# Layer 1's heads, its feed-forward and layer 2's attention in one instruction order instead of three stages

## The chip, the cores and the metric

The kernel runs on one core of a Trainium2 chip. The metric is the time of one execution in device microseconds; the median of several runs counts. The engines of a core are TensorE (PE in the profile, its weight loads PEld), VectorE (DVE), ScalarE (ACT), GpSimd (POOL) and SyncE (SP), which only issues DMA transfers here. Each has its own instruction stream, works it off in order, and waits on semaphores that the others count up.

## The reference, cut to what matters

The reference is a transformer of four layers on `x` of 4 x 256 tokens and 256 features. The change touches three blocks and what joins them:

```python
x = x + _L1_attn_ref(_layernorm(x), ...)     # causal, 16 heads of 16
x = x + _L1_xattn_ref(_layernorm(x), ctx)    # 16 heads of 16 over 256 context tokens, int8 rounding of x, o and weights
x = x + _L1_ffn_ref(_layernorm(x), w1, b1, w2, b2)
x = x + _L2_attn_ref(_layernorm(x), ...)     # causal, 32 query heads of 8 in 8 groups

def _bitlinear(x, w, b):                     # in _L1_ffn_ref, twice, 256 -> 1024 -> 256, gelu between
    xn = _layer_norm(x)
    xq = _activation_quant(xn)               # rounded to 127 steps of the row's maximum
    wq = _weight_quant(w)                    # -1, 0, 1 times a scale
    return jnp.einsum('bsd,fd->bsf', xq, wq) + b
```

## The kernel before

The 1024 tokens are eight tiles of 128 (`NT = 8`), two to a batch. The kernel is a list of stages (`STAGES`). Each stage has one function for each engine, and each function ends with a drain and a count of `stage done`; no engine begins a stage before the other four engines' counts of the stage before are in. Semaphore names are reused from stage to stage (`Signals.next_stage`). Three stages matter here.

`L1Heads` (a `SmallHeads`) holds layer 1's self attention and cross attention as eight batches of four steps `s` of four heads. Time is counted in quarters `q` of a step. For each quarter every engine's function has a fixed list of work: score matmuls (`pe_scores`, three steps ahead), maxima on VectorE (`maximum`), the probabilities' matmuls (`pe_probabilities`, L1107), the exponential on ScalarE (L1296), the values (`pe_values`, L1134) and VectorE's copy of them (L1187). Projections ("units") and the rest of a batch come by two tables, `units` and `plan`: "turn" (transposes L1152, then division and int8 rounding of the rows on VectorE, L1264 to L292), "flip" (L1156, copied by ScalarE for even tiles, L1301, and by VectorE for odd ones, L1195), "project" (L1161, then the addition to x, L1199, and the statistics of the next normalisation, L230 and L232), and four quarters later the normalisation itself (`apply_next`, L247). The last step of heads is `s = 31`, quarters 124 to 127; after it only turns (quarters 132, 134), flips (136, 138), projections (140, 142) and normalisations (144, 146) are left for the last two tiles; the projections of the two tiles before stand in quarters 124 and 126. The quarters end at 147.

`L1Ffn` is a software pipeline over the eight tiles with `PHASES = 14`: step `n` does phase `n - t` for each tile `t`, 21 steps in all (0 to 20). Phase 0: statistics on VectorE (L1574, L1576) and their root on POOL. Phase 1: row scaling on VectorE (`rows`, L1609 to L1617) and two rounding passes on ScalarE (L1625, L1629). Phase 2: transposes (L1540) and their copy (L1633). Phase 3: the hidden products (L1547), scaled with the bias on VectorE (L1587), Gelu and squares on ScalarE (L1637, L1641). Phase 5: the rows of 1024 on VectorE (L1609, L1611) and ScalarE's rounding (L1647, L1649). Phase 6: eight transposes (L1555), copied by L1653. Phase 7: the out product (L1561) and its addition to x (L1598). Phases 8 and 9: statistics and normalisation for layer 2 (L230, L247). Phase 11: its transposes and their copy (`turn` L254 and L255, `keep` L260).

`L2Attn`, again a `SmallHeads`, has four batches of eight steps of four heads. Its quarters begin at -24: a key projection (L1067, eight matmuls) and four query projections, each split in bf16 parts by copies on ScalarE and VectorE (L1232) with matmuls between them (L1052), two value projections (L1706), the first scores in quarter -12 (L1080, L1087), their maxima (L1249), the first probabilities in quarter 1 (L1099, L1107).

In PSUM (eight banks) the heads use banks 0 and 1 for scores, 2 and 3 for probabilities, 4 for values, 5 and 6 for units and 7 for the rest. The feed-forward uses 0 for the first transposes, 1 and 2 for the hidden products, 3, 4 and 5. In SBUF the heads and both following stages use the area `K` from column 0 on.

SyncE's stream: layer 2's q, k, v and out weights are loaded at the start of the feed-forward's stage (`L1Ffn.sp`), nine further weights and the split parts at the start of the attention's (`L2Attn.sp`, 3072 KB for the latter).

## Time and profile before

| | |
|---|---|
| median of 3 runs | 2391.01 us (2387.65 to 2399.65) |
| profiled execution | 2393.9 us, of which 2392.0 from the first to the last instruction |
| mean granted TensorE clock | 0.913 |
| busy share: PE, DVE, ACT, POOL | 85%, 66%, 48%, 36% |
| heads' last step of heads to the end of their stage | about 706 to 731.2 us |
| feed-forward's stage | 731.3 to 807.1 us |
| layer 2's attention to its first probabilities | 807.1 to 840.9 us |

The rows below are of three kinds. A windows row gives for a stretch of the span how long each engine was busy in it. A timeline row is one instruction, or several alike merged (x with their number), with its start, its length, and in brackets how long its engine had been idle before it and what ended that. A row of the chain is a piece of the work that ended last. The granted clock is a share of 2.4 GHz: 1.00 is that level and 0.50 is 1.2 GHz.

### The profile page before, as it was taken

How to read it: one execution, taken by the hardware profiler on the slowest of the kernel's cores; microseconds unless marked ns; L12 is line 12 of the kernel's file. 1: busy time of each engine (PE TensorE's matmuls, PEld its weight loads, DVE VectorE, ACT ScalarE, POOL GpSimd, SP SyncE). 2: the span in 40 equal slices, each digit the busy share in tenths (PEclk: the TensorE clock that was granted, in tenths of full speed). 3: DMA queues.
4: the chain of work that ended last, by engine and by line, in shares of the span. 5: the costliest groups of instructions: out<-in, count | busy, mean ns of one | idle time of the engine just before them, and what ended most of it. 6: DMA issues, size and time to landing. Idle time of an engine off the chain costs nothing.

```text
span 2392.0 us, 38312 instructions
## 1 busy us (share of the span) xinstructions
PE 2024.2 (85%) x13444; PEld 1458.8 (61%) x13521; DVE 1572.8 (66%) x4123; ACT 1153.3 (48%) x2563; POOL 855.2 (36%) x1374
## 2 busy tenths in 40 slices
PE   6999957899994699965678999689999999997991
PEld 4888844566652356542255677368778787774770
DVE  4866567356657555645587888677888888765433
ACT  2357637234436534427376656145655655552330
POOL 3247851011113211211000000166776767664445
PEclk9999978899996789975689999899999999998996
DMA  6124430000000300010000000311111111125543
GB/s 259 45 76 143 150 108 1 1 2 2 2 2 28 153 1 2 2 38 1 0 1 1 1 1 1 143 54 40 45 41 58 41 41 45 45 96 165 117 137 103
DMA packets 57694, 130.96 MB, mean 55 GB/s; under 512 B 6657, under 2 KB 23553, under 8 KB 55521
## 3 DMA queue, kind: packets, MB, share of 16 engines
q1 hardware_dynamic: 52656, 115.80, 14.2%
q0 software_dynamic: 4560, 12.46, 2.4%
q8 instruction: 109, 1.79, 0.3%
q14 instruction: 81, 0.66, 0.1%
q10 hardware_dynamic: 288, 0.26, 0.0%
HBM read 100.31 MB, written 26.08 MB: 53 GB/s over the span
## 4 chain that ended last, share of the span: by engine, by line
PE 69%; DVE 13%; ACT 8%; issue 4%; POOL 4%; DMA 1%; SPq 1%; POOLq 0%; DVEq 0%; ACTq 0%; another core or an unknown queue 0%
PE ps L1067 4%; PE ps L2164 4%; PE ps L2505 4%; PE ps L2183 4%; PE ps L2527 3%; PE ps L1107 3%; PE ps L2551 3%; PE ps L2959 3%; PE ps L1087 3%; PE ps L1134 2%; PE ps L2559 2%; PE ps L2496 2%; PE ps L2487 2%; PE ps L2488 2%; PE ps L601 2%
## 5 line engine op out<-in xcount | busy, mean ns | idle before, releaser
L2815 POOL TENSOR_TENSOR K<-K 128x512 f32<-128x512 f32 x128 | 144.9, 1132 | 147.2 <-DVE K L2612 147.1
L1296 ACT ACTIVATE K<-ps 128x768 f32<-128x768 f32 (+1 forms) x128 | 110.7, 865 | 153.2 <-PE ps L1107 151.4
L2212 DVE TENSOR_TENSOR_SCAN W<-W,ps 128x512 f32<-128x512 f32 x128 | 155.7, 1217 | 40.0 <-issue 24.5
L2164 PEld LDWEIGHTS ps<-K 128*128 128x128 f32 x1024 | 136.6, 196 | 64.9 <-issue 51.0
L2755 ACT ACTIVATE K<-ps,K 128x256 f32<-128x256 f32 x128 | 60.8, 475 | 212.9 <-DVE K L2596 212.9
L2607 DVE TENSOR_SCALAR K<-ps,K 128x128 f32<-128x128 f32 x384 | 130.8, 402 | 27.1 <-POOL K L2832 26.8
L2164 PE MATMUL ps<-K 128*128 128x128 f32 x1024 | 139.2, 280 | 6.8 <-DVE W L2212 6.8
L2801 POOL TENSOR_SCALAR K<-K 128x1 f32<-128x1 f32 x16 | 3.6, 224 | 371.3 <-DVE K L2662 368.9
L1339 POOL CAST K<-K 128x8 bf16<-128x8 f32 x64 | 14.9, 233 | 330.8 <-issue 157.2
L2183 PE MATMUL ps<-W,C 128*128 128x512 f32 x256 | 132.2, 598 | 0.7 <-DVE W L2220 0.6
L2505 PE MATMUL ps<-K 128*128 128x256 f32 x512 | 131.8, 380 | 0.7 <-ACT K L2774 0.7
L237 POOL TENSOR_SCALAR Z<-Z 128x1 f32<-128x1 f32 x80 | 19.4, 242 | 313.4 <-DVE Z L232 313.4
L1249 DVE TENSOR_REDUCE K<-ps 128x2 f32<-128x256 f32 x192 | 97.9, 552 | 43.1 <-PE ps L1087 41.8
L2596 DVE TENSOR_REDUCE K<-ps 128x2 f32<-128x512 f32 x128 | 87.7, 685 | 51.7 <-PE ps L2488 51.4
L2374 ACT ACTIVATE W<-K 128x510 f32<-128x510 f32 x128 | 87.4, 714 | 39.9 <-DVE W L2212 39.7
L729 POOL TENSOR_TENSOR K<-K 128x512 f32<-128x512 f32 x64 | 66.8, 1044 | 105.5 <-DVE K L677 105.5
L2551 PE MATMUL ps<-W,K 128*128 128x512 bf16 x352 | 89.9, 391 | 8.9 <-DMA W<-split_weights 5.1
L1232 ACT ACTIVATE K<-ps 128x512 bf16<-128x512 f32 (+1 forms) x80 | 44.7, 560 | 107.9 <-PE ps L1067 65.5
L1107 PE MATMUL ps<-K 32*128 32x256 bf16 (+1 forms) x1536 | 95.3, 256 | 0.8 <-ACT K L1296 0.8
L2505 PEld LDWEIGHTS ps<-K 128*128 128x128 f32 x512 | 87.3, 190 | 7.6 <-ACT K L2768 1.0
L702 ACT ACTIVATE K<-ps,K 128x256 f32<-128x256 f32 x64 | 30.3, 473 | 123.1 <-DVE K L654 122.8
L2527 PE MATMUL ps<-W,C 128*128 128x256 bf16 x720 | 88.2, 273 | 0.0
(524 smaller groups left out, 5757.9 us busy)
## 6 DMA issues: line engine op xcount, KB each, us to landing
W<-split_weights SPq DMA_DIRECT2D x32, 768.0 KB, 4.4
split_weights<-W SPq DMA_DIRECT2D x40, 384.0 KB, 2.6
W<-in_m SPq DMA_DIRECT2D x32, 256.0 KB, 4.7
results<-K SPq DMA_DIRECT2D x63, 128.0 KB, 2.4
W<-split_weights SPq DMA_DIRECT2D x1, 5376.0 KB, 16.7
W<-in_wproj SPq DMA_DIRECT2D x16, 256.0 KB, 3.0
W<-in_m SPq DMA_DIRECT2D x32, 128.0 KB, 5.6
W<-split_weights SPq DMA_DIRECT2D x1, 3072.0 KB, 20.3
```

What stands on the lines that cost most here:

```text
L1067: m = t.e.matmul(bank[:, i * 256:(i + 1) * 256], W[:, k, (c + i) * 128:(c + i + 1) * 128], x[:, k, b * 256:(b + 1) * 256], start=i == 0 an ...
L1107: m = t.e.matmul(self.probabilities_bank(b, j, k), y[:, k * 128:k * 128 + 128], x[:, q0:256], start=i == 0 and not self.causal(b), stop=i ...
L1249: m = e.tensor_reduce(to[:, :, i:i + 1], banks.rearrange("p (j k) -> p j k", j=2)[:, :, c0:c1], AX.X, ALU.max, negate=True)
L1296: e.activation(to, made, ACT.Exp, scale=self.SCALE).then_inc(*self.up("exp"))
L2164: m = e.matmul(ps[1 + 2 * (n % 2)][:, b * 128:(b + 1) * 128], self.dtuT[h][:, i, b * 128:(b + 1) * 128], self.diag[s % 4][:, b * 128:(b + ...
L2183: e.matmul(ps[4 + i][:, :], g.ident, self.y[(n - 3) % 5], start=False, stop=s == 15).then_inc(*sig.up("m total"))
L2212: e.tensor_tensor_scan(self.st[i % 3], self.a[i % 3], ps[1 + 2 * (i % 2)][:, :], 0.0, ALU.mult, ALU.add).then_inc(*sig.up("m scan"))
L2505: m = e.matmul(ps[6][:, 0:256], V[:, k, (i // 2) * 128:(i // 2 + 1) * 128], T[:, k * 256:(k + 1) * 256], start=k == 0, stop=k == 1)
L2527: m = e.matmul(ps[7][:, a * 256:(a + 1) * 256], self.o8[n % 3][:, i * 256 + a * 128:i * 256 + (a + 1) * 128], W[:, p * 512 + i * 256:p * 5 ...
L2551: m = e.matmul(bk[:, :], xs[:, cross, k, (j - 1) * 128:j * 128], W[:, p * 512:(p + 1) * 512], start=k == 0 and p == 0, stop=k == 1 and p == 2)
L2607: m = e.tensor_scalar(o[:, hs], ps[2 + u % 2][:, hs], mv[:, h, 0:1], r[:, h:h + 1], ALU.subtract, ALU.mult)
L2815: e.tensor_tensor(Pv, Pv, st[:, 4:6].unsqueeze(2).to_broadcast([128, 2, 256]), ALU.mult).then_inc(*sig.up("x scaled"))
```

## The change

The three stages become one, `Layers`, with one instruction order for all engines. The heads' quarters run as before; after the quarters named in `EARLY` one step of the feed-forward follows (step 0 after quarter 124, up to step 6 after quarter 145). Steps 7 to 11 follow the heads. From step 12 on (`BESIDE`) three quarters of layer 2's heads stand behind each step, so quarters -24 to 2 stand beside steps 12 to 20. The other quarters follow. The engine functions `pe`, `dve`, `act` and `pool` of `SmallHeads` and `L1Ffn` are split in a part before the loop (`dve_begin` and so on) and one for a single quarter or step (`pe_at` and so on); what they issue for it is unchanged. The feed-forward moves to buffers and PSUM banks that the heads no longer use (its first transposes to bank 2, hidden products to 0 and 1, the last transposes to 7; buffers in `W` and at the end of `K`), with waits that these are free. The loads of layer 2's q, k, v and out weights wait for the heads' last unit, the nine further loads and the split parts for the last tile's normalisation and its transposes.

```diff
-    LEAD, NB = 3, B
+    LEAD, NB, NAME = 3, B, "heads "
...
-        a, spare, more = Area(g.K, 0, WKCOLS), Area(g.W, 11264, 14336), Area(g.W, 2048, 4096)
+        a, spare, more = Area(g.K, 0, 17460), Area(g.W, 11264, 14336), Area(g.W, 2048, 4096)
...
-    def __init__(self, g):
-        self.g, self.sig, self.ps = g, g.sig, g.ps
-        a = Area(g.K, 0, 20020)
-        self.st, self.sc = a.new(NT, 2, 16), a.new(NT, 2, 4)
-        self.r1, self.rq, self.rqT = a.ring(2, 256), a.ring(3, 256, dt=BF16), a.ring(3, 2, 128, dt=BF16)
-        self.rh, self.rt = a.ring(4, 1024), a.ring(3, 1024)
-        self.squares = a.new(1024, dt=BF16)
-        self.rg, self.rgT = a.ring(3, 1024, dt=BF16), a.ring(3, 8, 128, dt=BF16)
+    def __init__(self, g, heads):
+        self.g, self.sig, self.ps, self.heads = g, g.sig, g.ps, heads
+        a, b, c = Area(g.W, 4096, 9216), Area(g.W, 14336, 19456), Area(g.K, 17460, 20020)
+        self.rh = a.ring(4, 1024)
+        self.st, self.sc, self.r1 = a.new(NT, 2, 16), a.new(NT, 2, 4), a.ring(2, 256)
+        self.rt, self.squares, self.rg = b.ring(3, 1024), b.new(1024, dt=BF16), b.ring(3, 1024, dt=BF16)
+        self.rq, self.rqT, self.rgT = c.ring(3, 256, dt=BF16), c.ring(3, 2, 128, dt=BF16), c.ring(3, 8, 128, dt=BF16)
...
-    def steps(self):
-        for step in range(NT + self.PHASES - 1):
-            for t in range(max(0, step - self.PHASES + 1), min(NT, step + 1)):
-                yield t, step - t
-
-    def sp(self, d):
+    STEPS = NT + PHASES - 1
+
+    def tiles(self, step):
+        return [(t, step - t) for t in range(max(0, step - self.PHASES + 1), min(NT, step + 1))]
+
+    def sp(self, d, heads):
+
+        d.wait_ge(heads.s("unit"), len(heads.made))
         for name in ("wq2", "wk2", "wv2", "wo2"):
             self.g.load(d, name)
 
-    def pe(self, t):
+    def pe_at(self, t, step):
         g, sig, ps, e = self.g, self.sig, self.ps, t.e
-        t.wait_ge(sig["w ternary"], 64)
-        for i, ph in self.steps():
+        for i, ph in self.tiles(step):
             if ph == 2:
                 t.wait_ge(sig["l1f rows"], i + 1)
                 t.wait_ge(sig["l1f kept"], i)
-                pb = ps[0].bitcast(BF16)
+                t.wait_ge(self.heads.s("exp"), 2 * self.heads.N)
+                pb = ps[2].bitcast(BF16)
                 for k in range(2):
                     m = e.transpose(pb[:, k * 128:(k + 1) * 128], self.rq[i % 3][:, k * 128:(k + 1) * 128], g.identb)
                 m.then_inc(*sig.up("l1f turned"))
             elif ph == 3:
+                t.wait_ge(sig["w ternary"], 64)
                 t.wait_ge(sig["l1f kept"], i + 1)
                 t.wait_ge(sig["l1f biased"], 2 * i)
+                t.wait_ge(self.heads.s("maximum"), 2 * self.heads.N)
                 for c in range(2):
                     for k in range(2):
-                        m = e.matmul(ps[1 + c][:, :], self.rqT[i % 3][:, k, :], self.w1[:, k, c * 512:(c + 1) * 512],
+                        m = e.matmul(ps[c][:, :], self.rqT[i % 3][:, k, :], self.w1[:, k, c * 512:(c + 1) * 512],
                                      start=k == 0, stop=k == 1)
                     m.then_inc(*sig.up("l1f hidden"))
...
+                t.wait_ge(self.heads.s("quad kept"), self.heads.N)
...
-                g.norms[6].turn(t, i, ps[5])
-
...
+    NAME = "heads of 8 "
+
     def sp(self, d):
+
+        nx = self.g.norms[6]
+        d.wait_ge(self.sig[nx.name + " xnT"], nx.tbase + NT)
+        d.wait_ge(self.sig["l1f x"], NT)
...
+        t.wait_ge(self.sig[g.norms[6].name + " xnT"], g.norms[6].tbase + 2 * b + 2)
...
+class Layers:
+
+
+
+    EARLY = {124: 0, 126: 1, 129: 2, 132: 3, 136: 4, 140: 5, 145: 6}
+    BESIDE = 12
+
+    def __init__(self, g):
+        self.g, self.sig = g, g.sig
+        self.heads = L1Heads(g)
+        self.ffn = L1Ffn(g, self.heads)
+        self.attn = L2Attn(g)
+
+    def order(self):
+
+        for q in self.heads.quarters:
+            yield "heads", q
+            if q in self.EARLY:
+                yield "ffn", self.EARLY[q]
+        first, behind = max(self.EARLY.values()) + 1, list(self.attn.quarters)
+        for step in range(first, self.ffn.STEPS):
+            yield "ffn", step
+            if step >= self.BESIDE:
+                for q in behind[3 * (step - self.BESIDE):3 * (step - self.BESIDE) + 3]:
+                    yield "attn", q
+        for q in behind[3 * (self.ffn.STEPS - self.BESIDE):]:
+            yield "attn", q
+
+    def heads_ended(self, eng):
+
+        h, nx = self.heads, self.g.norms[5]
+        eng.wait_ge(h.s("rest"), max(h.made_rest.values()))
+        eng.wait_ge(h.s("kept"), len(h.number))
+        eng.wait_ge(h.s("quads"), h.N)
+        eng.wait_ge(h.s("quad kept"), h.N)
+        eng.wait_ge(h.s("logits"), 2 * h.N)
+        eng.wait_ge(h.s("exp"), 2 * h.N)
+        eng.wait_ge(h.s("unit"), len(h.made))
+        eng.wait_ge(h.s("parts"), h.N // 2)
+        eng.wait_ge(h.s("quantised"), NT)
+        eng.wait_ge(self.sig[nx.name + " xn"], nx.base + NT)
+
+    def banks_free(self, t, q):
+
+        nx = self.g.norms[6]
+        if q >= -4 * self.attn.LEAD:
+            t.wait_ge(self.sig["l1f biased"], 2 * NT)
+        if q >= -1:
+            t.wait_ge(self.sig["l1f kept"], NT)
+            t.wait_ge(self.sig["l1f hidden kept"], NT)
+            t.wait_ge(self.sig["l1f x"], NT)
+            t.wait_ge(self.sig[nx.name + " xnT"], nx.tbase + NT)
+
+    def sp(self, d):
+        self.heads.sp(d)
+        self.ffn.sp(d, self.heads)
+        self.attn.sp(d)
+
+    def pe(self, t):
+        for stage, n in self.order():
+            if stage == "heads":
+                self.heads.pe_at(t, n)
+            elif stage == "ffn":
+                self.ffn.pe_at(t, n)
+            else:
+                if n == self.attn.quarters[0]:
+                    self.heads_ended(t)
+                self.banks_free(t, n)
+                self.attn.pe_at(t, n)
+
...
-STAGES = [(1, L0Attn), (3, L0Cross), (5, L1Heads), (6, L1Ffn), (7, L2Attn), (8, L2Cross), (9, L2Moe),
+STAGES = [(1, L0Attn), (3, L0Cross), (7, Layers), (8, L2Cross), (9, L2Moe),
...
```

The functions `dve`, `act` and `pool` of `Layers` follow the same order as its `pe`.

## Rows read from the trace of the kernel before

**Rows 1.** The page's part 1, busiest engine: busy us, share, instructions.
```profile
PE 2024.2 (85%) x13444; PEld 1458.8 (61%) x13521; DVE 1572.8 (66%) x4123; ACT 1153.3 (48%) x2563; POOL 855.2 (36%) x1374
```

**Rows 2.** Windows: length, busy PE, PEld, DVE, ACT, POOL, granted clock, DMA share, GB/s.
```profile
706.00:731.40 25.40, 16.34 (x96) 8.63 (x92) 10.92 (x33) 3.46 (x4) 3.29 (x8) 0.63 0.00 1
731.40:762.00 30.60, 11.68 (x49) 5.16 (x50) 24.18 (x71) 21.51 (x36) 11.98 (x24) 0.52 0.15 54
762.00:793.00 31.00, 18.11 (x93) 10.29 (x94) 27.79 (x69) 29.96 (x49) 10.76 (x24) 0.67 0.00 1
793.00:807.10 14.10, 8.12 (x52) 5.18 (x49) 8.01 (x23) 9.06 (x13) 3.33 (x8) 0.76 0.01 2
807.10:825.80 18.70, 11.85 (x48) 8.09 (x49) 3.54 (x10) 6.62 (x11) 1.88 (x6) 1.00 0.95 372
825.80:840.90 15.10, 10.05 (x87) 4.58 (x88) 7.87 (x16) 2.22 (x4) 1.93 (x10) 0.71 0.37 145
840.90:858.00 17.10, 16.75 (x133) 8.66 (x133) 6.40 (x12) 4.65 (x6) 1.92 (x10) 0.55 0.00 1
```

**Rows 3.** Timeline, the heads' last quarters: start us, length us, instruction, [idle before].
```profile
713.55 0.42 DVE L1199 TENSOR_TENSOR X<-ps,X 128x256 f32<-128x256 f32 x1 [0.99 <-PE ps L1161]
...
714.47 0.18 DVE L232 BATCH_NORM_AGGREGATE Z<-Z 128x2 f32<-128x6 f32 x1
...
714.53 1.02 ACT L1296 ACTIVATE K<-ps 128x1024 f32<-128x1024 f32 x1 [3.27 <-PE ps L1107]
...
717.98 0.26 DVE L1264 RECIPROCAL K<-ps 128x16 f32<-128x16 f32 x1 [0.49 <-PE ps L1152]
...
720.23 0.25 DVE L1264 RECIPROCAL K<-ps 128x16 f32<-128x16 f32 x1
...
723.94 2.08 PE L1161 MATMUL ps<-W,K 128*128 128x256 f32 x4 [0.58 <-DVE K L1195]
```

**Rows 4.** Timeline, feed-forward, the first instructions of some steps.
```profile
733.14 0.80 DVE L1609 TENSOR_SCALAR K<-W,K 128x256 f32<-128x256 f32 x1 [1.06 <-POOL K L1666]
...
735.13 0.42 DVE L1574 BATCH_NORM_STATS2 K<-W 128x6 f32<-128x256 f32 x1
...
735.31 0.60 ACT L1625 ACTIVATE K<-K,Z 128x256 f32<-128x256 f32 x1 [13.21 <-DVE K L1581]
...
745.44 1.54 DVE L1587 SCALAR_TENSOR_TENSOR K<-ps,K,C 128x512 f32<-128x512 f32 x2 [2.43 <-PE ps L1547]
...
749.04 0.78 DVE L1609 TENSOR_SCALAR K<-K 128x1024 f32<-128x1024 f32 x1
...
755.28 0.78 DVE L1609 TENSOR_SCALAR K<-K 128x1024 f32<-128x1024 f32 x1
...
761.98 0.48 DVE L1598 SCALAR_TENSOR_TENSOR X<-ps,K,X 128x256 f32<-128x256 f32 x1
```

**Rows 5.** Timeline, feed-forward from its step 12 on.
```profile
795.64 1.03 PE L1555 MATMUL ps<-Cb,K 128*128 128x128 bf16 x8 [1.85 <-ACT K L1649]
...
798.89 1.15 ACT L1649 ACTIVATE K<-K,Z 128x1024 bf16<-128x1024 f32 x1
...
802.25 1.05 PE L1561 MATMUL ps<-W,K 128*128 128x256 bf16 x8 [0.69 <-ACT K L1653]
...
806.67 0.38 ACT L260 ACTIVATE K<-ps 128x256 f32<-128x256 f32 x1 [0.79 <-PE ps L255]
```

**Rows 6.** Timeline, layer 2's attention until its first probabilities.
```profile
807.14 1.99 PE L1067 MATMUL ps<-K,W 128*128 128x256 f32 x8 [0.51 <-ACTq L3426]
...
815.27 1.89 PE L1067 MATMUL ps<-K,W 128*128 128x256 f32 x8
...
825.82 0.32 PEld L1080 LDWEIGHTS ps<-Cb 128*128 128x128 bf16 x2
...
840.89 0.82 PE L1107 MATMUL ps<-K 32*128 32x256 bf16 x8
```

**Rows 7.** The chain that ended last, a projection in layer 2's second batch.
```profile
852.63 3.69 PE ps L1067 x8
```

More of the change, by code:

```diff
@@ new lines, in pe_at @@
+    def pe_at(self, t, q):
+        s, p, second = q // 4, q % 4 // 2, q % 2
+        if not second and 0 <= s + self.LEAD < self.N:
+            self.pe_scores(t, s + self.LEAD, p)
+        if second and 0 <= s < self.N:
+            self.pe_probabilities(t, s, p)
+        for u, kind, b, c, n in self.units.get(q, ()):
+            if n == 0:
+                if u >= 2:
+                    self.wait_part(t, u - 2, self.last[u - 2])
+                m = self.unit(t, kind, b, c, self.ps[5 + u % 2])
+            else:
+                self.wait_part(t, u, n - 1)
+                t.wait_ge(self.s("minus"), 1)
+                m = t.e.matmul(self.ps[5 + u % 2][:, :], self.minus[self.levels(kind, b)[n - 1][2]], self.part(u, kind, b, c, n - 1),
+                               start=False, stop=True, skip_group_check=True)
+            m.then_inc(*self.up("unit"))
+        if q % 4 == 1 and 0 <= s - 1 < self.N:
+            self.pe_values(t, s - 1)
+        for kind, b, c, u in self.plan.get(q, ()):
+            t.wait_ge(self.s("kept"), u)
+            m = self.pe_rest(t, kind, b, c)
+            if kind != "norm":
+                m.then_inc(*self.up("rest"))
@@ L1310, in pool, with pool_begin @@
+    def pool_begin(self, p):
         e = p.e
@@ L1563, in pe, with dve_at @@
             elif ph == 11:
-                g.norms[6].turn(t, i, ps[5])
-    def dve(self, v):
+                t.wait_ge(self.heads.s("kept"), len(self.heads.number))
+                g.norms[6].turn(t, i, ps[7])
+    def dve_at(self, v, step):
         g, sig, ps, e = self.g, self.sig, self.ps, v.e
         xn = g.norms[5].xn
-        for i, ph in self.steps():
+        for i, ph in self.tiles(step):
             s0, s1, c0, c1 = self.st[:, i, 0, :], self.st[:, i, 1, :], self.sc[:, i, 0, :], self.sc[:, i, 1, :]
@@ L1618, in rows, with act_at @@
         v.wait_ge(v.own, v.n)
-    def act(self, a):
+    def act_at(self, a, step):
         g, sig, ps, e = self.g, self.sig, self.ps, a.e
-        for i, ph in self.steps():
+        for i, ph in self.tiles(step):
             if ph == 1:
@@ L1655, in act, with pool_at @@
             elif ph == 11:
-                g.norms[6].keep(a, i, ps[5])
-    def pool(self, p):
+                g.norms[6].keep(a, i, ps[7])
+    def pool_at(self, p, step):
         g, sig, e = self.g, self.sig, p.e
-        for i, ph in self.steps():
+        for i, ph in self.tiles(step):
             s0, s1 = self.st[:, i, 0, :], self.st[:, i, 1, :]
```

205 lines of the change are left out of this document (109 added, 96 removed).

## The prediction, made before the change was run

> **What bounds the kernel now.** I read the page first. TensorE is busy 85% of the span [rows 1], but that is a mean over stages, and the change touches only the stretch from the heads' last quarters to the first quarters of layer 2's attention. So I cut that stretch into windows [rows 2] and ask of each which engine has no room. In the heads' tail (706 to 731.4) VectorE works 10.9 of 25.4 us and ScalarE 3.5: a chain of small steps from engine to engine, with room on both. In the feed-forward's filling steps (to 762) VectorE works 24.2 of 30.6. In its full steps (to 793) ScalarE works 30.0 of 31.0 and VectorE 27.8: ScalarE is the bound and there is nothing to win. From 793 to 807 the pipeline drains, all engines below two thirds. Then layer 2's projections (to 825.8) are again a chain: VectorE 3.5 and ScalarE 6.6 of 18.7 us. From 825.8 on TensorE and VectorE hand one score bank pair to and fro. The change lays the filling steps over the heads' tail, and the draining steps over the projections. Both overlaps are of latency-bound work with latency-bound work on in-order engines, so what counts is not the sum of busy times but what each inserted piece makes the next one wait for.
>
> **The change, part by part: the front.** I follow VectorE, which is the slower engine here, from quarter 126. Nothing before it changes: step 0 is two short statistics instructions. Quarter 126's addition starts at 713.55 and its statistics end at 714.65 [rows 3], so an addition with statistics costs 1.1.
>
> Step 1 is new behind it. One tile's row scaling takes 2.0 (733.14 to 735.13), and the next tile's statistics 0.6 [rows 4]: 2.6 together. ScalarE, in order, has to do its part of step 1 before the exponential of quarter 127. The scale is ready at 716.7, ScalarE's two passes take 1.1, so that exponential starts at about 717.9 where it started at 714.53 [rows 3]: 3.4 late. TensorE's values and VectorE's copy of them queue behind it. Step 2 stands behind quarter 129 and adds 2.6 on VectorE, of which 0.4 fell into idle time. So quarter 132's row work starts at 723.6, not 717.98: 5.6 late. It takes 2.3 (717.98 to 720.23) [rows 3].
>
> From here on the rest is a sum on VectorE: 725.9; step 3, as long as step 4 was before (745.44 to 749.04, 3.6) [rows 4]: 729.5; quarter 134's rows 2.3: 731.8; step 4, 3.6 and 0.4 of wait for its hidden products, which stand behind the flip of quarter 136 on TensorE: 735.8; quarter 138's copy 0.4: 736.2; wait for the projection of quarter 140, 2.1 of TensorE [rows 3] and the hand-over, 2.5: 738.7; addition and statistics 1.1: 739.8; step 5 6.2 (749.04 to 755.28) [rows 4]: 746.0; quarter 142 1.1 and the normalisation of quarter 144 0.4: 747.5; step 6 6.7 (755.28 to 761.98): 754.2; the last normalisation 0.4: 754.6. Before, step 7 began at 761.98 [rows 4]. The front gives 7.4. The whole tail disappears as a stage of its own, but its work does not: from 706 to 762 VectorE has 35.1 us of work [rows 2].
>
> Its bounds: from 713.55 to 762 VectorE works about 34 of 48.4 us (35.1 of [rows 2], less about 1.4 that stand before 713.55); its chains of dependent short instructions leave some 4 of gaps which nothing fills. So the front gives 11 at the very most. At the least: if each inserted step costs its old time including its waits, only steps 0 to 2 (731.4 to about 739.3) fall into idle time, less the 5.6 by which they delay quarter 132: 2.
>
> **Steps 7 to 11** keep their pace: ScalarE is full [rows 2].
>
> **The tail.** TensorE finished step 12 at 796.67 and ScalarE at 800.04 [rows 5]; both come 7.4 earlier, 789.3 and 792.6. The 27 quarters of the next heads go in threes behind steps 12 to 20. The first key projection (2.0 [rows 6]) can run while ScalarE is in step 12, but its copy waits for ScalarE until 792.6, 1.3 later than on an idle engine. From this projection to the next but one took 8.1 before (807.14 to 815.27) [rows 6]. Now TensorE has in addition step 13 (a turn 0.4, the out product 1.05, eight transposes 1.03 [rows 5]) and step 14 (0.4 and 1.05). About 0.7 of step 13 lies in the time in which TensorE would wait for the copy. Sum: 789.3 + 8.1 + 1.3 + 2.5 - 0.7 + 1.5 = 802.0 for the second query projection. Step 13's copy on ScalarE (1.0) goes ahead of the keys' last copies, but these are done before the chain needs them. From there to the first scores took 10.6 (815.27 to 825.82) [rows 6], plus 0.4 for one turn that is in nobody's shadow: 813.0. The old time was 825.82. From the scores to the first probabilities took 15.1 (to 840.89) [rows 6]. The last turns lie in TensorE's waits for the maxima; I add 0.5 for a maximum that comes behind the last normalisation. So by the chain alone the first probabilities start at 828.6, 12.3 earlier. The draining stage from 796.67 to 807.05 [rows 5] was 10.4 long, and I get 5 of it: the rest is paid back as TensorE work inside the new chain.
>
> **Edits costed at nothing.** The Q, K, V, out weights of layer 2 are loaded earlier, the nine big loads and the split parts later by at most the length of the draining steps; the first reader of the latter is a stage away, and DMA is idle before it. The new waits (the heads' counters, the free banks) are met: each is counted up at least a step before. The exponential's table is still left once and taken again once, since the last exponential stands ahead of step 3 and the first new one behind step 10. POOL works under 40% everywhere here [rows 2]. Two stage borders go, 0.2 us.
>
> **The clock** is the term that no row settles. The granted clock was 1.00, the level of 2.4 GHz, in the projections (807 to 825.8), though TensorE was busy only 11.9 of 18.7 us, and between the two levels (0.76) in the drain before it [rows 2]. The same eight matmuls take 1.89 at the high level [rows 6] and 3.69 in the stretch of 0.55 [rows 7, 2]. Now the projections start at 789.3, where the clock was at the low level. TensorE is busier here than in the old drain, so I expect the high level after the first or second projection. One slow projection is half hidden by ScalarE, the second is not: 1.5 lost. Bounds: nothing, if it rises at once; if it never does, five projections at 1.8 more (9.0, 1.3 of it hidden), the value projections 1.0, three pairs of scores 0.5 each: 11.
>
> Here the Trainium skill (TensorE: Matmul & The Clock Gate, Part 1: The HAM clock gate) speaks for the change's second half. It says that the slow level is the default and that sustained work on the array releases it. By it the filled gaps would keep the clock up and the 1.5 would not be lost. The trace agrees that the projections ran at 1.00, but it also shows a busy array at 0.55 from 840.9 to 858 (16.8 of 17.1 us) [rows 2], so I keep the 1.5.
>
> **Sum:** 12.3 - 1.5 = 10.8 earlier, and nothing after this stretch changes. The profiled execution took 2393.9 us (span 2392.0); the median of the runs is 2391.0. I take the gain off the median: **2380.2 us**, 0.45% less. A measurement of this kernel can tell about 0.5% (12 us) from no change, so the forecast lies just inside.
>
> **Rivals.**
> *Full overlap.* The inserted steps fit into idle time almost everywhere: front 11, tail 10 (the whole drain). For it: VectorE's 10.9 of 25.4 and ScalarE's 3.5 in the tail [rows 2]. Against it: the 3.4 us by which the exponential of quarter 127 is late, and TensorE's in-order work at each step border. 21 less: 2370. With half of the difference to my sum, 2375.
> *The in-order engines give it back.* Each inserted step waits for a result that is just being made, and the quarter behind it waits too. Front 2, tail 1: 2388. For it: the waits of 2.4 and 1.06 that the filling steps showed [rows 4].
> *Slower, by the clock.* The low level holds from 790 through the projections (11 lost, which leaves 1.3 of the gain) and lasts longer under the first quarters that follow. There TensorE is busy 16.75 of 17.1 us at 0.55 [rows 2]: the work would take half the time at full clock. If as much of such work again is done at the low level, 8.5 more: 2398. It decides from about 3 us of saturated work at the low level beyond the stretch that was slow before. Against it: the projections alone brought 1.00 before.
>
> **How the numbers follow.** Forecast 0.54, full overlap 0.24, given back 0.13, slower by the clock 0.09. The forecast's own range is 2375 to 2386, and two fifths of it lie beyond 0.5%. So faster by over 0.5%: 0.24 and 0.21 of the forecast, 0.45. Slower by over 0.5% (above 2403) takes two such stretches: 0.05. Within: 0.50. The range reaches to full overlap on one side and to the case that gives it back on the other: 2369 to 2391.
>
> **What the new profile would show.** The exponential of quarter 127 3 to 4 us after 714.5; the first Gelu near 727, not 741; step 7 on VectorE near 755; the full steps still 7.1 apart; the first key projection near 789 to 790, and 12 to 14 us from it to the second query projection, where it was 8.1; the first scores near 813 to 815; the first probabilities near 829 to 831; granted clock 1.00 from about 795 to 820; after it the same pace to the end. Wrong would be: step 7 not before 759 (the front's chain), or projections of 3.7 us each after 797 (the clock), or a low stretch behind the first probabilities much longer than 17 us, or a wait for a weight in the stages after.

## The result and the profile after

The changed kernel's median is 2371.82 us (nine runs, 2366.25 to 2385.55), against 2391.18 us (nine runs, 2387.65 to 2403.75) for the kernel before on the same chip. The ratio is 0.9921, with a 95% interval of 0.9903 to 0.9939: 19.4 us, or 0.8%, faster. The forecast was 2380.2, a gain of 10.8. Its direction was right, the time lies in its range, and the gain was sized at little more than half; the case "faster by over 0.5%", which came, had been given 0.45.

The profiled execution took 2366.25 us (span 2364.3), the fastest of its nine. The one of before took 2393.9 (span 2392.0), near the middle of its own. So the two profiles differ by 27.7 us, more than the kernels do, and the first task is to say which part belongs to the change. The page's part 1 has the same work as before, instruction for instruction on TensorE [rows 1]; its matmuls are busy 17 us less:

```profile
PE 2007.2 (85%) x13444; PEld 1451.7 (61%) x13521; DVE 1571.2 (66%) x4123; ACT 1152.4 (49%) x2563; POOL 857.4 (36%) x1374
```

Three names are used from here on. The front is the stretch on VectorE from quarter 126's addition to the first instruction of step 7, the tail the stretch from there to the first probabilities on TensorE, and the low level a granted clock of 0.50 (1.2 GHz). Windows of the changed kernel, with the columns of [rows 2]: the heads' last quarters with steps 1 to 6 beside them; the full steps; the draining steps beside layer 2's projections; from its first scores to its first probabilities; the stretch behind. The fence ends with three shorter stretches of the same core, of which the granted clock is what matters.

```profile
704.30:742.70 38.40, 19.14 (x102) 10.21 (x102) 31.74 (x97) 23.41 (x40) 13.82 (x29) 0.73 0.00 0
742.70:773.50 30.80, 16.90 (x91) 9.53 (x94) 28.16 (x71) 29.82 (x48) 11.16 (x24) 0.68 0.00 1
773.50:802.50 29.00, 21.21 (x96) 15.10 (x96) 10.63 (x31) 13.73 (x21) 5.39 (x14) 0.81 0.00 1
802.50:817.00 14.50, 9.95 (x89) 4.75 (x88) 7.69 (x15) 3.37 (x7) 1.93 (x10) 0.71 0.55 201
817.00:834.00 17.00, 16.61 (x154) 8.80 (x154) 8.42 (x16) 5.25 (x7) 2.16 (x12) 0.75 0.92 367
...
788.60:807.90 19.30, 13.80 (x94) 9.34 (x93) 8.26 (x19) 8.24 (x17) 2.05 (x5) 1.00 0.00 0
808.00:824.90 16.90, 13.69 (x111) 5.48 (x111) 7.11 (x14) 3.76 (x5) 3.86 (x20) 0.52 0.94 368
825.20:832.00 6.80, 6.41 (x70) 3.84 (x69) 3.92 (x8) 2.22 (x3) 0.00 (x0) 0.97 1.02 397
```

Where the heads' tail had VectorE at 10.9 of 25.4 us and the filling steps at 24.2 of 30.6 [rows 2], one stretch now has it at 31.74 of 38.40. The full steps are as long as before.

The timeline of the same stretch (VectorE, ScalarE and one TensorE row), to set beside [rows 3] and [rows 4]. L1200 is the addition that was L1199, L1265 the reciprocal that was L1264, L1299 the exponential that was L1296, L1619 the row scaling that was L1609, L1608 the addition that was L1598:

```profile
704.35 0.42 DVE L1200 TENSOR_TENSOR X<-ps,X 128x256 f32<-128x256 f32 x1 [0.61 <-PE ps L1160]
705.37 0.38 DVE L1619 TENSOR_SCALAR W<-W 128x256 f32<-128x256 f32 x1
...
707.70 0.51 ACT L1639 ACTIVATE K<-W,Z 128x256 bf16<-128x256 f32 x1
708.12 1.00 ACT L1299 ACTIVATE K<-ps 128x1024 f32<-128x1024 f32 x1
...
709.17 1.60 PE L1133 MATMUL ps<-K,W 128*32 128x256 f32 x16 [3.88 <-ACT K L1299]
...
713.62 0.25 DVE L1265 RECIPROCAL K<-ps 128x16 f32<-128x16 f32 x1
...
719.34 0.23 DVE L1265 RECIPROCAL K<-ps 128x16 f32<-128x16 f32 x1
...
725.33 0.39 DVE L1196 COPY K<-ps 128x256 f32<-128x256 f32 x1
...
725.77 1.26 PE L1160 MATMUL ps<-W,K 128*128 128x256 f32 x4 [2.66 <-DVE K L1196]
...
727.08 0.42 DVE L1200 TENSOR_TENSOR X<-ps,X 128x256 f32<-128x256 f32 x1 [1.36 <-PE ps L1160]
...
728.10 0.78 DVE L1619 TENSOR_SCALAR W<-W 128x1024 f32<-128x1024 f32 x1
...
736.14 0.80 DVE L1619 TENSOR_SCALAR W<-W 128x1024 f32<-128x1024 f32 x1
...
742.72 0.48 DVE L1608 SCALAR_TENSOR_TENSOR X<-ps,W,X 128x256 f32<-128x256 f32 x1
```

Read it with quarter 126's addition as zero. It stands at 704.35, and stood at 713.55 [rows 3], and but for step 0's two short statistics the instructions ahead of it are the same in both kernels: these 9.2 us are not the change's. Most of them are older than the heads' end. The addition of layer 1's first projection on VectorE shows it, in the kernel before and in the changed one:

```profile
513.92 0.42 DVE L1199 TENSOR_TENSOR X<-ps,X 128x256 f32<-128x256 f32 x1 [1.76 <-PE ps L1161]
...
507.80 0.42 DVE L1200 TENSOR_TENSOR X<-ps,X 128x256 f32<-128x256 f32 x1 [1.76 <-PE ps L1160]
```

So 6.1 us were there 200 us ahead of the change, and nearly all of that arises between 350 and 480 us, where the two executions had another granted clock. The same window of both, before and after:

```profile
395.00:460.00 65.00, 44.97 (x260) 29.46 (x263) 25.86 (x64) 25.22 (x39) 9.07 (x30) 0.76 0.00 1
...
395.00:460.00 65.00, 44.67 (x318) 29.89 (x320) 26.10 (x65) 26.26 (x41) 10.74 (x39) 0.89 0.00 1
```

The other 3.1 us come near the end of the heads, where the stretch at the low level was 3.4 us long in this execution and 10.2 in that of before. From the zero of quarter 126's addition, the exponential of quarter 127 starts 3.77 later (0.98 before), TensorE waits 3.88 for it, quarter 132 begins after 9.3 us, quarter 134 after 15.0, and step 7 after 38.37. That last figure was 48.43 before [rows 3, 4].

TensorE's timeline from the first projection of layer 2 on, to set beside [rows 6]:

```profile
776.22 2.75 PE L1066 MATMUL ps<-K,W 128*128 128x256 f32 x8
...
783.08 3.62 PE L1066 MATMUL ps<-K,W 128*128 128x256 f32 x8
...
786.92 1.61 PE L1570 MATMUL ps<-W,K 128*128 128x256 bf16 x8
788.37 0.61 PE L1563 MATMUL ps<-Cb,W 128*128 128x128 bf16 x8
...
791.51 1.89 PE L1066 MATMUL ps<-K,W 128*128 128x256 f32 x8
...
802.50 0.38 PE L1079 MATMUL ps<-Cb 128*128 128x256 bf16 x2
...
816.99 0.61 PE L1098 MATMUL ps<-Cb 128*128 128x256 bf16 x2
...
827.89 1.35 PE L1066 MATMUL ps<-K,W 128*128 128x256 f32 x5
```

The first projection has moved to 33.5 us behind step 7, where it was 45.2 [rows 4, 6]. The third comes 15.3 us behind the first (8.1 before), since step 13's out product and transposes, and step 14, stand between the second and the third, and since the first two run at 2.75 and 3.62 us, not 1.99 and 1.89. From step 7 to the first probabilities it is 74.3 us; in the profile of before it was 78.4, from 761.98 to the first pair of products of L1099:

```profile
840.35 0.61 PE L1099 MATMUL ps<-Cb 128*128 128x256 bf16 x2
...
852.56 3.76 PE L1067 MATMUL ps<-K,W 128*128 128x256 f32 x8
```

So of the 27.7 us between the two profiles 9.2 lie ahead of the change. 10.1 come from its front and 4.1 from its tail. The rest, 4.3, lies behind it, 1.3 of that between the first probabilities and the next batch's first projection (10.9 us, and 12.2 before, 840.35 to 852.56), where the stretch at the low level was 17.1 us long here and 23.9 there. Two profiles alone give the change 14.2 us. The timed runs give it 19.4. That difference is what most of the experiments are about.

### The profile page after: what moved, and what is told of

The parts are those of the page before. It is cut to its first block, busy times and chain, and to the rows that moved or that the text cites. A ratio compares the mean times of both kernels' runs of the same rounds, so it can differ in the third digit from the quotient of the medians.

```text
span 2364.3 us, 38312 instructions
## 1 busy us (share of the span) xinstructions
PE 2007.2 (85%) x13444; PEld 1451.7 (61%) x13521; DVE 1571.2 (66%) x4123; ACT 1152.4 (49%) x2563; POOL 857.4 (36%) x1374
## 4 chain that ended last, share of the span: by engine, by line
PE 68%; DVE 14%; ACT 7%; issue 5%; POOL 4%; DMA 1%; SPq 1%; POOLq 0%; another core or an unknown queue 0%; DVEq 0%; ACTq 0%
PE ps L2632 4%; PE ps L2291 4%; PE ps L1066 4%; PE ps L2310 4%; PE ps L2654 3%; PE ps L2678 3%; PE ps L1106 3%; PE ps L3086 3%; PE ps L1086 3%; PE ps L1133 2%; PE ps L2686 2%; PE ps L2623 2%; PE ps L2614 2%; PE ps L2615 2%; PE ps L601 2%
## 5 line engine op out<-in xcount | busy, mean ns | idle before, releaser
L1299 ACT ACTIVATE K<-ps 128x768 f32<-128x768 f32 (+1 forms) x128 | 110.7, 865 | 145.5 <-PE ps L1106 143.8
L1106 PE MATMUL ps<-K 32*128 32x256 bf16 (+1 forms) x1536 | 93.8, 253 | 0.8 <-ACT K L1299 0.8
```

Of the source, the lines that this page charges most:

```text
L1106: m = t.e.matmul(self.probabilities_bank(b, j, k), y[:, k * 128:k * 128 + 128], x[:, q0:256], start=i == 0 and not self.causal(b), stop=i ...
L1299: e.activation(to, made, ACT.Exp, scale=self.SCALE).then_inc(*self.up("exp"))
```

## The experiments

No kernel leaves work out. The "spare matmuls" of some are products whose results nothing reads.

**One half at a time, neither, and one step later.**

e1_front_only keeps the early steps and puts all of layer 2's quarters behind the feed-forward:

```
-    BESIDE = 12
+    BESIDE = 21
```

> Feed-forward steps 0 to 6 in the heads' last quarters as in the change, but layer 2's quarters all behind step 20 (BESIDE = 21). Theory A (two chains, each shortened by its own overlap, as in the prediction; the sizes as the changed kernel's trace has them): this keeps the front's 10 us, so about 2381, ratio 0.996; the addition of quarter 126 to VectorE's step 7 takes 38 us as in the changed kernel, and the projections run from the drain's end at the high clock. Theory B (the gain beyond 10.8 us is the clock's, because work beside the drain keeps TensorE busy): front alone gives the predicted 7 or less, 2384 or more. Theory C (the front gives nothing that the tail does not need): 2390.

e2_tail_only keeps the overlap behind step 12 and starts the feed-forward after the heads:

```
-    EARLY = {124: 0, 126: 1, 129: 2, 132: 3, 136: 4, 140: 5, 145: 6}
+    EARLY = {}
...
-        first, behind = max(self.EARLY.values()) + 1, list(self.attn.quarters)
+        first, behind = max(self.EARLY.values(), default=-1) + 1, list(self.attn.quarters)
```

> All feed-forward steps behind the heads (EARLY empty), layer 2's quarters beside steps 12 to 20 as in the change. Theory A: the tail alone gives 3 to 5 us, about 2387, ratio 0.998; from the last transposes of the draining pipeline to the first probabilities about 41 us where it was 44. Theory B: the tail is the larger half and this kernel is 9 or more faster, 2382 or less, with a shorter low stretch of the clock behind the first scores (17 us, not 25).

e3_neither makes both edits: the new code in the old order.

> One stage with neither overlap (EARLY empty, BESIDE = 21): only the other banks and buffers, the earlier loads and the missing stage borders remain. Both theories: within 3 us of the kernel before, 2388 to 2392. A rival (the borders, buffers and banks carry part of the gain): 2384 or less.

e4_step1_after_127 lets the exponential of quarter 127 go ahead of step 1:

```
-    EARLY = {124: 0, 126: 1, 129: 2, 132: 3, 136: 4, 140: 5, 145: 6}
+    EARLY = {124: 0, 127: 1, 129: 2, 132: 3, 136: 4, 140: 5, 145: 6}
```

> The changed kernel with feed-forward step 1 behind quarter 127 in place of 126, so that ScalarE's exponential of quarter 127 stands ahead of it. Theory A (the prediction's step: that exponential is 3.4 us late and everything to quarter 132 with it): the exponential starts 1.0 us after the addition of quarter 126 instead of 3.8, quarter 132's rows 2.5 to 3 us earlier, the kernel 2 to 3 us faster than the changed one, 2369. Rival (VectorE is full from there on and takes the time back): same as the changed one, 2372.

All four ran on one chip, where the kernel before had a median of 2395.27 us in 24 runs (2385.97 to 2403.67). The last two columns are read from each kernel's profile, from quarter 126's addition to step 7 and from there to the first probabilities:

| kernel | median (runs) | ratio, 95% | front | tail |
|---|---|---|---|---|
| front only | 2381.04 (8) | 0.9939, 0.9917 to 0.9961 | 39.5 | 84.2 |
| tail only | 2389.59 (12) | 0.9965, 0.9944 to 0.9985 | 48.1 | 72.3 |
| neither | 2393.54 (12) | 1.0002, 0.9982 to 1.0022 | 48.1 | 84.7 |
| step 1 after 127 | 2371.25 (6) | 0.9905, 0.9873 to 0.9937 | 36.4 | 73.7 |

The new code in the old order is the kernel before, as far as 12 runs can tell (5 us either way): what the change moves in memory and in its waits shows no cost. The halves add up within their intervals: 0.9939 times 0.9965 is 0.9904, and the whole is 0.9921 with an interval that holds it. The front is worth 9 to 10 us by the profiles (48.1 to 48.5 in the old order, 37.4 to 39.5 in the new) and 14.6 by its ratio, of which the interval, 9.3 to 19.9, just holds the other reading. The tail is worth 8.4 by its ratio (3.6 to 13.4). The forecast had 7.4 and 3.4. Neither half gives back what the other wins. Against what was expected of these kernels: front only came out at the 2381 of theory A, but its projections did not run at the high level, as that theory had it (3.62 and 3.16 us for the first two). Tail only was to be 3 to 5 us faster; its ratio gives more, its median 5.7.

The step behind quarter 127 confirms the reading of the late exponential. It starts 0.98 after the addition again, as in the kernel before; ScalarE's timeline of that run has it ahead of step 1's pass, and the addition was at 717.37:

```profile
718.35 1.02 ACT L1299 ACTIVATE K<-ps 128x1024 f32<-128x1024 f32 x1 [3.57 <-PE ps L1106]
720.08 0.60 ACT L1635 ACTIVATE W<-W,Z 128x256 f32<-128x256 f32 x1 [0.71 <-DVE W L1591]
```

Step 7 comes 2.0 us sooner after quarter 126 than in the change (36.4 for 38.4). In the total, 2 us can't be told from nothing by six runs: 0.9905 against 0.9921 with overlapping intervals, and 2371.25 us where 2369 was expected.

**The kernel before, twice more.** The table already says something that the first profile did not: neither and front only, both with the old tail, took 84.7 and 84.2 us for it, not 78.4. To see whether that is the new code or the execution, the kernel before was run and profiled again, unchanged, as g2_before_again and g3_before_again.

> The kernel before, profiled again. The claim: the profile that the prediction used had layer 2's first projections at the high clock (1.99 and 1.89 us), which is not how this kernel mostly runs; here the first two take 3.2 to 3.7 us and the way from VectorE's step 7 to the first probabilities is 84 us, not 78. Rival: 1.9 and 78 again, and the low level in the two kernels with the old order (front only, neither) came from their other buffers and borders.

> The same once more, for the same question: the first two projections 3.2 to 3.7 us by the claim, 1.9 by the rival. The low stretch near the end of the heads (10 us in the first profile, 3 to 14 in the later ones) should be there again, with another length.

They took 2398.30 and 2402.91 us, with 83.4 and 81.6 us from step 7 to the first probabilities. Windows of the first of them, the feed-forward's draining steps, the first two projections, and the rest of the projections:

```profile
791.20:805.80 14.60, 10.15 (x50) 6.14 (x48) 7.75 (x22) 8.17 (x12) 3.12 (x8) 0.50 0.01 2
...
807.40:816.30 8.90, 7.37 (x17) 5.04 (x18) 1.44 (x7) 1.20 (x2) 1.87 (x6) 0.52 0.88 342
816.40:829.60 13.20, 8.30 (x35) 5.09 (x34) 2.08 (x3) 5.43 (x9) 0.00 (x0) 1.00 1.03 412
```

and TensorE's timeline of it, with an out product and the first three projections:

```profile
800.88 1.89 PE L1561 MATMUL ps<-W,K 128*128 128x256 bf16 x8 [0.69 <-ACT K L1653]
...
807.39 3.78 PE L1067 MATMUL ps<-K,W 128*128 128x256 f32 x8 [0.51 <-ACTq L3426]
...
813.71 3.01 PE L1067 MATMUL ps<-K,W 128*128 128x256 f32 x8
...
818.82 1.89 PE L1067 MATMUL ps<-K,W 128*128 128x256 f32 x8
```

The same out product took 1.05 and the first projections 1.99 and 1.89 in the first profile [rows 5, 6], with a granted clock of 0.76 in the drain and 1.00 behind it [rows 2]. Here the drain is at 0.50, the low level, and the rise comes only at 816. Nothing in the code differs. In g3_before_again the first projection took 3.44 and the second 1.89; with neither it was 3.62 and 3.24, with the front only 3.62 and 3.16. Over the five profiles of the old tail without spares (78.4, 83.4, 81.6, 84.7, 84.2) the mean is 82.5 us, and the profile on which the forecast was built is the shortest of the five. The other four, though, were taken in executions whose time lies above the median: 2398.30, 2402.91, 2400.17 for neither (median 2393.54) and 2398.36 for front only, the longest of its eight. So the mean may lie above what a median execution has. Against that, a short time does not need a short tail: one kernel of the old order below, with spare matmuls in its drain, was profiled at 2387.39 us and has 82.2 us there, and its quarter 126 at 705.07. Over the five of the new tail with no spares between step 7 and the first scores (74.3, 72.3 with the tail only, 73.7 with step 1 behind 127, and 73.3 and 73.4 in two kernels below) the mean is 73.4, and they lie within 2 us.

**Is the gain only the clock's?** If a longer stay at the high level were what the change gains, a kernel that is held there should gain nothing by the new order. Spare matmuls were put where TensorE idled:

```
+    def fill(self, t, bank, n):
+        x = self.g.identb.rearrange("p (i n) -> p i n", i=1).to_broadcast([128, 4, 128])
+        for _ in range(n):
+            t.e.matmul(self.g.ps[bank][:, :].rearrange("p (i n) -> p i n", n=128), self.g.identb, x, start=True, stop=True,
+                       skip_group_check=True)
```

f1_fill_scores puts three of them behind seven of the quarters that make layer 2's first scores, in the changed kernel:

```
+                if n in (-12, -10, -8, -6, -4, -2, 0):
+                    t.wait_ge(self.sig["l1f kept"], NT)
+                    self.fill(t, 2, 3)
```

> The changed kernel with three spare matmuls (128x512 bf16, identity by identity, result never read) behind the score matmuls of quarters -12, -10, ... 0 of layer 2's heads, where TensorE waits for the maxima. It tests whether the granted clock behind the first scores is a term of time that the kernel's own gaps set. Clock theory: the low stretch of 17 to 24 us there goes, TensorE was full in about 16 us of it, so 7 to 8 us faster than the changed kernel (about 2364), and the spread of the runs shrinks. Rival (the clock follows something else, or the spare work costs what it gives): 2372 or more, low stretch still there.

f3_fill_heads puts two to four behind eleven of the heads' last quarters (quarter: bank and number), each time with a wait for the last maxima, and from quarter 130 on for the last exponentials, which read those banks:

```
+    FILL = {117: (0, 2), 119: (0, 4), 127: (0, 4), 128: (0, 4), 130: (3, 2), 131: (3, 2), 133: (3, 4), 135: (3, 4), 137: (3, 3), 139: (3, 3), 141: (3, 3)}
```

> The changed kernel with two to four spare matmuls behind eleven of the heads' quarters from 117 to 141, where TensorE waits for VectorE or ScalarE. Clock theory: the low stretch of 3 to 14 us at the end of the heads goes (full TensorE work there, worth up to 5 us) and the projections of quarters 140 and 142 take 1.1 instead of 2.1: 3 to 5 us faster than the changed kernel, 2368. Rival (spare matmuls at full TensorE cost more than they give): 2373.

f4_fill_all has both, and four behind each of the feed-forward's steps 10 to 12:

```
+                if n in (10, 11, 12):
+                    self.fill(t, 6, 4)
```

> Both sets of spare matmuls, and four more behind each of the feed-forward's steps 10, 11 and 12, in the changed order. Clock theory: the sum, 12 us faster than the changed kernel, about 2360, runs within 6 us of one another. Rival: no better than the better one of the two parts.

f5_neither_fill_all is the old order with the same spares, and four behind each of steps 2 to 20:

```
+                if n in range(2, 21):
+                    self.fill(t, 6, 4)
```

> The old order (EARLY empty, BESIDE = 21) with the same spare matmuls in the heads and the scores, and four behind each of the feed-forward's steps 2 to 20, so that the clock stays high where it matters in this order too. What is left between this kernel and the changed order with spare matmuls is the gain without the clock. Theory A (both overlaps shorten chains, 9 to 10 us in front and 4 to 5 in the tail): 14 us above it, about 2374. Theory B (half of the measured 19 us is the clock that stays high longer in the changed order): 10 us or less above it, about 2370. Theory C (the clock is no part at all): 19 above it.

All four ran on one chip (kernel before: 2393.28 in 15 runs). The last column is the time at the low level between 640 and 900 us:

| kernel | median (runs) | ratio, 95% | front | tail | low level |
|---|---|---|---|---|---|
| f1 | 2368.04 (5) | 0.9897, 0.9863 to 0.9931 | 38.6 | 73.3 | 71.7 |
| f3 | 2373.36 (5) | 0.9914, 0.9881 to 0.9947 | 37.4 | 73.4 | 64.8 |
| f4 | 2365.20 (5) | 0.9879, 0.9845 to 0.9913 | 38.1 | 72.1 | 37.5 |
| f5, old order | 2383.93 (11) | 0.9953, 0.9935 to 0.9972 | 47.0 | 81.2 | 37.5 |

For comparison, the changed kernel had 71.7 us at the low level there, the kernel before 102.4, 112.6 and 119.5 in its three profiles.

f4 and f5 spend the same 37.5 us at the low level, and the new order is still 18.7 us faster by the medians (15.8 by the means). Ten or less had been expected if half of the gain were the clock's, fourteen if both overlaps shorten chains by what had been read so far, nineteen if the clock had no part. The two ratios leave some 9 us either way (an estimate from their intervals), so that ten lies at the edge of what they allow, and fourteen and nineteen can't be told apart. That counts against the clock as the main source of the gain, but less cleanly than it looks, since the spares cost the old order something too. Windows of f5, from step 7 to the first scores and from there to the first probabilities; and below them those of f4, where the first begins with the draining steps:

```profile
750.70:818.50 67.80, 47.56 (x256) 27.81 (x255) 40.84 (x100) 45.15 (x70) 15.70 (x37) 0.90 0.30 116
818.50:831.90 13.40, 12.01 (x106) 5.51 (x105) 8.04 (x16) 2.33 (x4) 1.94 (x10) 1.00 0.26 99
```

```profile
779.40:807.50 28.10, 19.11 (x102) 13.59 (x101) 12.37 (x36) 14.36 (x21) 5.00 (x14) 0.94 0.00 0
807.50:820.70 13.20, 12.17 (x110) 5.93 (x109) 8.24 (x17) 3.48 (x7) 1.93 (x10) 1.00 0.46 173
```

The clock is at 0.90 and above in both, and from the scores on it takes 13.4 and 13.2 us. In f5 all projections take 1.89, and yet its tail is 81.2, longer than the 78.4 of the first profile of before.

g4_neither_fill_drain asks for this cost alone: the old order, with four spares behind each of steps 10 to 20 and none elsewhere.

```
+                if n in range(10, 21):
+                    self.fill(t, 6, 4)
```

> The old order in one stage (neither overlap) with four spare matmuls behind each of the feed-forward's steps 10 to 20 and nowhere else: TensorE is busy in the drain. If the low clock of the first projections costs the old order 5 to 6 us, this gives it back: all projections at 1.9, step 7 to the first probabilities 78 to 80 us instead of 84.7, about 2388 against 2394, ratio to before 0.997 to 0.998. Rival (the old order mostly runs its projections at the high level anyway, or the spare work costs as much): 2393 or more, ratio 1.000.

It ran at 2394.71 us (12 runs; kernel before 2392.78 in 17), ratio 1.0005, 0.9986 to 1.0024: the expected gain did not come. TensorE's timeline shows both sides of the bargain:

```profile
799.36 2.75 PE L1826 MATMUL ps<-Cb 128*128 128x512 bf16 x12
801.95 1.24 PE L1066 MATMUL ps<-K,W 128*128 128x256 f32 x5
```

The first projection is at the high level (so are the four behind it, 1.89 each), but it stands behind twelve spares, 2.75 us of them, and comes 48.8 us after step 7, where it came after 45.2, 47.1 and 47.1 in the three profiles of the kernel before. What the clock gives in the projections the spares take in the drain, in part at least: 82.2 us for the tail, against 84.7 with neither in its one profile and a total that is the same. In the drain the old order has nothing useful to put where the spares go; the new order has the projections.

The spares behind the first scores are different. f1's timeline of TensorE:

```profile
807.54 0.81 PE L1826 MATMUL ps<-Cb 128*128 128x512 bf16 x3
...
819.80 0.38 PE L1098 MATMUL ps<-Cb 128*128 128x256 bf16 x2
820.11 0.50 PE L1106 MATMUL ps<-K 32*128 32x256 bf16 x8
...
827.51 1.35 PE L1066 MATMUL ps<-K,W 128*128 128x256 f32 x5
```

They lie in TensorE's waits for VectorE's maxima, and there is no low stretch any more: the window from 806.5 to 827.5 has a granted clock of 1.00. From the first probabilities to the next batch's projection it takes 7.7 us, where it took 10.9 in the change and 11.2 to 12.2 in every other profile with the low level there; the eight products of L1106 take 0.50, not 0.82. From the first scores on that is 21.0 us for 25.4, 4.4 won where 7 to 8 had been expected. In the total, f1's 2368.04 lies between the 2364 of the clock theory and the 2372 of its rival, and its ratio can't be told from the change's (0.9897 and 0.9921, overlapping intervals). The spares in the heads did what they were put there for (none of the four kernels that have them shows the low stretch ahead of quarter 126's addition, of 3.4 to 13.7 us in all others), but the ratio of f3 shows no gain from it: 2373.36 us, its rival's 2373 and not the 2368 of the clock theory. Nor did the sum come: f4 was to run at 2360 with all runs within 6 us, and ran at 2365.20 with runs from 2363.11 to 2373.61.

**The best version.** g1_best is f4 with step 1 behind quarter 127 and spares behind step 9 too:

```
-    EARLY = {124: 0, 126: 1, 129: 2, 132: 3, 136: 4, 140: 5, 145: 6}
+    EARLY = {124: 0, 127: 1, 129: 2, 132: 3, 136: 4, 140: 5, 145: 6}
...
+                if n in (9, 10, 11, 12):
+                    self.fill(t, 6, 4)
```

> The changed order with all spare matmuls (heads, feed-forward steps 9 to 12, scores) and step 1 behind quarter 127. Clock theory and the in-order term add: 1 to 2 us below the kernel with all spare matmuls, 2363 to 2366, ratio to before 0.987 or 0.988. Rival: the two do not add, 2368 or more.

2365.48 us (6 runs, 2364.03 to 2369.70), ratio 0.9887, 0.9864 to 0.9909. Front 36.1, tail 71.6, 34.1 us at the low level. f4 (0.9879) and g1 can't be told apart. By medians both are some 6 us below the changed kernel, by ratios 8 to 10, and their ratios' intervals just overlap with its own, so that this further step is likely, not certain. Against the kernel before both intervals lie well below 1.

## Why the prediction was right in direction and short in size

**The front: 7.4 forecast, 9 to 10 measured.** The chain was followed rightly and every term came out a little shorter. With quarter 126's addition as zero: quarter 132 forecast at 10.05, found at 9.3 (the exponential 3.8 behind the zero, so 2.8 later than before, not 3.4); quarter 134 at 15.95, found at 15.0; the copy of quarter 138 at 22.25, found at 21.0; the addition of quarter 140 at 25.15, found at 22.7; step 7 at 41.05, found at 38.37. The largest single miss is the wait for quarter 140's projection: 2.5 forecast with the 2.08 of [rows 3] in it, 1.36 found, since the four matmuls ran faster (1.26). The price of that row came from a stretch at the low level. The full steps kept their pace (30.2 us for steps 7 to 11, 31.1 before), and the exponential's delay went where it was said to go, into TensorE's wait. Undoing it gave the 2.0 us of e4.

**The tail's chain: right in length.** From step 7 to the first scores the forecast gives 58.4 and 1.5 for the clock, 59.9. Found: 59.7, to their weight load as the forecast counts. That it fits so closely is partly luck: two errors of 1.2 or so offset each other: the first projection came 1.2 sooner behind step 7 than forecast, and the third 15.3 behind the first, outside the 12 to 14 that were named. From the scores to the probabilities (counted to the second of their products, L1106 at 817.52, as the forecast counted) it took 15.1 us for 15.6.

**The clock: the term that failed.** The forecast took 1.5 off the gain, because the new projections might begin at the low level while those of before ran at the high one. The first half of the thought was right: the two first ones took 2.75 and 3.62 us, and measured from step 7 the clock was at 1.00 from 45 us on (forecast 40) until 66 (forecast 65). The second half was read from one execution. In the other profiles of the old order, those of g2, g3, e1 and e3, the old projections begin at the low level as well, and the drain ahead of them is at 0.50, not 0.76 [rows 2]. That makes the old tail 81.6 to 84.7 us where the forecast had 78.4. The step of the prediction that failed is its sentence that the granted clock was 1.00 in the projections, used as a property of the kernel: it was a property of that run. So the clock gave something to the change, where 1.5 had been taken off. Its worst case for the clock, 11 lost, is also added up wrongly: 9.0 with 1.3 of it hidden, 1.0 and 1.5 make 10.2.

**The sum, set right:** 10.8, and 2.7 for the front (38.4 for 41.05), and 1.6 for the new tail (73.4 for 75.0, counted to the first of the probabilities' products, the clock's 1.5 included), and 4.1 for the old tail (82.5 for 78.4): 19.2, against 19.4 measured. The last term rests on five profiles that spread over 6 us, four of them of executions that took longer than the median, and is known to 1 or 2 us at best; that the sum comes out so near is no proof of it. The first two terms do not depend on it.

Here the Trainium skill (TensorE: Matmul & The Clock Gate, Part 1: The HAM clock gate) had been set against the trace: the slow level is the default, sustained work releases it, and so filled gaps would help. The trace agrees as to the projections, which run at 1.00 from 788.1 on (in the window from 788.6 TensorE is busy 13.8 of 19.3 us). It agrees less behind them: at 808.6 the level falls, and in the window from 808.0 TensorE is busy 13.7 of 16.9 us at 0.52.

**The rivals.** Full overlap was priced at 21 less, with front 11 and tail 10. The result lies nearer to that number (2370) than to the forecast's, and the front, 9 to 10, lies halfway between its 11 and the 7.4. Its reason for the tail, that the whole drain disappears, did not come: the new tail ran as the forecast's chain said, and the time was won against an old tail that is longer than it had looked. "The in-order engines give it back" (2388, front 2 and tail 1) is refuted by e1 and e2, whose intervals (9.3 to 19.9 and 3.6 to 13.4 us) leave both out. "Slower, by the clock" (2398) is refuted: the low level ended at 788.1, and the low stretch behind the first scores was 17.1 us (17.1 to 23.9 in the profiles of the new tail without spares there), against 17.1 to 27.3 with the old tail.

**What stays open.** Why an execution's clock falls early or late is not explained: the same code showed 102.4, 112.6 and 119.5 us at the low level between 640 and 900 us. How long the old tail is in a median execution was not measured, since most profiles are of longer ones. How much of the gain is the level's and how much the order's can't be separated by the spare matmuls, which cost time in the old order's drain. That the old tail is longer when its drain and projections run slow is shown by their durations; that the new order is less exposed to it is what five profiles show (72.3 to 74.3), and no experiment forced it.

## What to carry to other kernels

Before a term that hangs on the granted clock goes into a sum, profile the unchanged kernel again: one execution's level is a sample, and here the sample was 4 us off in a stretch of 80. Two profiles also differ ahead of the change (here by 9.2 us), so set both to zero at the last instruction that the change leaves alone. In the front, two chains bound by latency laid over each other on in-order engines kept four fifths or more of what the idle time allowed (9 to 10 of at most 11); the inserted piece that delayed a releaser (the exponential) is seen at once in the wait of the engine behind it and is moved by one quarter. Spare matmuls gained 4.4 us in the one stretch where TensorE waited for the maxima (f1), nothing that shows in the total in the heads' waits (f3), and nothing where real work stood queued behind them (g4).

## What the hardware showed that was not expected

- **The granted clock differs between executions of one program.** Runs of the kernel before lay between 2385.97 and 2403.67 us on one chip, in step with their mean granted clock: 0.917 at about 2386, 0.910 at about 2400. Much of this lies ahead of anything that was changed: over the fourteen profiles, quarter 126's addition stands between 703.7 and 719.5 us, with the same work ahead of it but for step 0 and the spares of quarters 117 and 119.
- **A full TensorE can be at the low level, and one that idles for a third of the time at the high level.** From 840.9 to 858 it was busy 16.75 of 17.1 us at 0.55, and in the projections 11.85 of 18.7 at 1.00 [rows 2]. In the first stretch products over 32 rows alternate with ones over 128, the second holds products over 128 only; that this is the reason is not shown. In f1, three spare matmuls of 128x512 behind each of seven quarters came with no low stretch at all (1.00 from 806.5 to 827.5).
